# A fourth decay buffer for a state-space scan, placed in SBUF, and side work moved to later scans

## What is computed

```python
mod = silu(c) @ W_ada + b_ada;  shift, scale, gate = split(mod, 3)
h = layernorm(x, gamma, beta) * (1 + scale) + shift;  h = h[:, perm]
xm, z = split(h @ W_in, 2);  xm = silu(conv4(xm) + conv_b)          # 1024 channels
dtr, B, C = split(xm @ W_xp, [64, 80]);  dt = softplus(dtr @ W_dt + b_dt)
for t in rows:                                                       # state: 1024 channels x 16
    state = state * exp(dt_t * A) + (dt_t * x_t) * B_t;  y_t = sum_s state * C_t
out = x + gate * (((y + xm * D) * silu(z)) @ W_out)[inverse]
```

## Time and profile before

| | |
|---|---|
| median of 3 runs | 3013.91 us |
| the profiled execution | 3009.61 us, span 3007.8 us, mean granted TensorE clock 0.949 |
| DVE busy | 2466.3 us (82% of the span) |
| PE busy | 2648.0 us (88%) |
| POOL busy | 1883.4 us (63%) |
| ACT busy | 1621.8 us (54%) |
| stretch of the scans, 1030.7 to 2951 us | 1920.3 us, DVE busy in 1844.98, POOL 1676.82, PE 1633.54, ACT 1324.89 |

### The profile page before, as it was taken

One profiled execution on the slowest core, in us unless ns is written; L12 is line 12 of the kernel. 1 busy time (PEld: TensorE's weight loads), 2 busy tenths in 40 slices (PEclk: granted clock), 3 DMA queues, 4 the chain that ended last, 5 costly groups with the idle time before them and its releaser, 6 DMA issues. The chain is left out here.

```text
span 3007.8 us, 31819 instructions
## 1 busy us (share of the span) xinstructions
PE 2648.0 (88%) x10790; PEld 1499.2 (50%) x10790; DVE 2466.3 (82%) x3111; ACT 1621.8 (54%) x2444; POOL 1883.4 (63%) x822
## 2 busy tenths in 40 slices
PE   7999999999999877988988988988888897897974
PEld 3555555555555354554554554455455455454542
DVE  3566556666656599999999999999999998999993
ACT  1221322331332576776875875776676687586550
POOL 0131121222122396897998899799799799889991
PEclk9999999999999878999989999999999998998976
DMA  6102231231233444555664575665575566566653
GB/s 216 36 28 85 69 106 42 91 112 36 91 112 116 135 98 97 118 126 119 151 148 122 143 164 115 146 158 120 133 161 130 133 148 147 126 142 137 171 122 75
DMA packets 261604, 355.39 MB, mean 118 GB/s; under 512 B 21597, under 2 KB 115937, under 8 KB 261434
## 3 DMA queue, kind: packets, MB, share of 16 engines
q1 hardware_dynamic: 202024, 246.38, 26.8%
q0 software_dynamic: 55680, 105.93, 20.1%
q10 hardware_dynamic: 3730, 0.96, 0.2%
HBM read 215.56 MB, written 71.58 MB: 95 GB/s over the span
## 5 line engine op out<-in xcount | busy, mean ns | idle before, releaser
L2073 POOL TENSOR_TENSOR hs<-slots,b_wide 128x2048 f32<-128x2048 f32 x255 | 1270.5, 5011 | 142.8 <-PE bank L1589 142.6
L2267 DVE TENSOR_TENSOR_SCAN hs<-bank,hs 128x512 f32<-128x512 f32 x1024 | 1224.5, 1215 | 30.3 <-ACT bank L1846 25.3
L1846 ACT ACTIVATE bank<-dt,decay 128x512 f32<-128x512 f32 x1022 | 698.6, 691 | 540.7 <-DVE hs L2267 538.5
L1589 PE MATMUL bank<-ident,hs 128*128 128x128 f32 x4096 | 676.1, 295 | 240.1 <-DVE acc L2285 181.0
L1589 PEld LDWEIGHTS bank<-ident,hs 128*128 128x128 f32 x4096 | 515.1, 150 | 724.3 <-issue 264.0
L2285 DVE SCALAR_TENSOR_TENSOR acc<-bank,c_t,acc 128x512 f32<-128x512 f32 x772 | 566.4, 734 | 43.0 <-PE bank L1589 40.2
L1541 PE MATMUL bank<-h_t,w_in 128*128 128x512 f32 x1024 | 510.8, 608 | 1.4 <-ACT h_t L1764 1.2
L2121 POOL DMA_DIRECT2D acc<-scaled x252 | 291.2, 1155 | 49.2 <-DMA acc<-scaled 35.0
L982 POOL TENSOR_TENSOR y_rs<-y_var,mhalf 128x8 f32<-128x8 f32 x8 | 15.8, 1972 | 393.5 <-DVE y_var L355 393.5
L1641 PE MATMUL bank<-w_y,values 128*128 128x512 f32 x512 | 253.0, 600 | 1.3 <-DVE values L2389 1.3
L800 PE MATMUL bank<-z_t,w_k 128*128 128x512 f32 x512 | 223.0, 594 | 4.3 <-DVE k_t L1009 3.2
(11 more groups left out here) (180 smaller groups left out, 3344.3 us busy)
## 6 DMA issues: line engine op xcount, KB each, us to landing
b_wide<-b_rows SPq DMA_DIRECT2D x256, 256.0 KB, 3.6
acc<-scaled POOLq DMA_DIRECT2D x252, 256.0 KB, 5.3
w_in<-in_L_cond_W_in SPq DMA_DIRECT2D x128, 256.0 KB, 4.4
res<-in_x SPq DMA_DIRECT2D x8, 2048.0 KB, 10.0
h_tiles<-h_t SPq DMA_DIRECT2D x56, 256.0 KB, 2.8
h_in<-h_tiles SPq DMA_DIRECT2D x56, 256.0 KB, 4.1
x_rows<-w_part POOLq DMA_DIRECT2D x28, 512.0 KB, 6.8
x_rows<-res SPq DMA_DIRECT2D x6, 2048.0 KB, 7.3
```

The lines of the kernel that those rows point to most:

```text
L1589: last = nc.tensor.transpose(bank[:, j * P:(j + 1) * P], hs[:, slot, j, t * P:(t + 1) * P], ident[:, :])
L1846: nc.scalar.activation(decay_banks[N % 3][:, :], dt[:, H % 2, j, :], ACT.Exp, scale=g.decay[:, 4 * (H % 2) + j, s:s + 1]).then_inc(da_read ...
L2073: nc.gpsimd.tensor_tensor(hs[:, U % RING, :, :], slots[:, H % SLOTS, :, :], b_wide[:, U % B_RING, :].unsqueeze(1).to_broadcast([P, 4, CHUNK]),
L2267: nc.vector.tensor_tensor_scan(block, decay_banks[N % 3][:, :], block, 0.0, ALU.mult, ALU.add).then_inc(scanned, 1)
```

## The change

`decay_banks` gets a fourth entry, `decay_tile`, which lies in SBUF where the other three are PSUM banks. Since a unit has four scans, the fourth scan of every unit, 256 in all, reads its decay from SBUF, and the other three keep a bank of their own. ACT now issues the decay of scan n + 4 at step n; it still waits until scan n has ended. The addition to the second half's step sizes (`ADD_DT_AT`) moves on POOL from unit 7 to 9. ACT's `shift` moves from step 14 to 18, and the four normalisations, which stood together at 15, stand one each at 19, 20, 21 and 22, each behind its own column of `shift`. The transposes, the modulations and the first product by W_in follow by one or two steps, the second silu of z by one, and the first product waits for each modulated tile by itself instead of for the last three together. `raw`, the place of the moments, now lies in columns of `cols` that layer 0 has used up.

```diff
+DECAY_RING = 4
-H_AT = (21, 22, 22, 28)
+H_AT = (23, 24, 24, 28)
-XM_AT = (30, 33, 42, 51, 62, 63, 66, 69)
+XM_AT = (31, 33, 42, 51, 62, 63, 66, 69)
-SILU_Z_AT = (104, 2)
+SILU_Z_AT = (104, 3)
-NORM_AT = 15
-MOD_AT = (26, 27, 27, 33)
+NORM_AT = (19, 20, 21, 22)
+MOD_AT = (27, 28, 29, 33)
-ADD_DT_AT = (28, 7)
+ADD_DT_AT = (28, 9)
-SHIFT_AT = 14
+SHIFT_AT = 18
-        g.raw = sb("raw1", [P, CT, 6])
+        g.raw = g.cols[:, 0:6 * CT].rearrange("p (t s) -> p t s", t=CT)
-def rows_normed_by_act(nc, g, n, it):
-    need(nc.scalar, g.shift_ready, CT * n)
-    for t in range(CT):
-        nc.scalar.activation(g.rows[:, t, :], ...).then_inc(g.normed, 1)
+def rows_normed_by_act(nc, g, n, t):
+    need(nc.scalar, g.shift_ready, CT * (n - 1) + t + 1)
+    nc.scalar.activation(g.rows[:, t, :], ...).then_inc(g.normed, 1)
...
-        state_banks, decay_banks, work_banks = banks[0:2], banks[3:6], [banks[6], banks[7], banks[2]]
+        decay_tile = sb("decay_tile", [P, CHUNK])
+        state_banks, decay_banks, work_banks = banks[0:2], [*banks[3:6], decay_tile], [banks[6], banks[7], banks[2]]
...
-                    if stage == "xm" and m == 0:
-                        for i in range(KD)[-place.ring:]:
-                            need(pe, *read_by(place, "h", i))
                 for k in ks:
+                    if stage == "xm" and m == 0:
+                        need(pe, *read_by(place, "h", k))
...
-                need(act, scanned, N - 2)
-                nc.scalar.activation(decay_banks[N % 3][:, :], dt[:, H % 2, j, :], ACT.Exp,
+                need(act, scanned, N - (DECAY_RING - 1))
+                nc.scalar.activation(decay_banks[N % DECAY_RING][:, :], dt[:, H % 2, j, :], ACT.Exp,
...
-                    if N + 3 < BLOCKS * BATCH:
-                        decays(N + 3)
+                    if N + DECAY_RING < BLOCKS * BATCH:
+                        decays(N + DECAY_RING)
...
-                nc.vector.tensor_tensor_scan(block, decay_banks[N % 3][:, :], block, 0.0, ALU.mult, ALU.add).then_inc(scanned, 1)
+                nc.vector.tensor_tensor_scan(block, decay_banks[N % DECAY_RING][:, :], block, 0.0, ALU.mult, ALU.add).then_inc(scanned, 1)
```

More of the change, by code:

```diff
@@ L447, in rows_shift_by_act @@
         nc.scalar.activation(g.shift[:, t:t + 1], g.rs[:, t:t + 1], ACT.Copy, scale=g.mean_neg[:, t:t + 1]).then_inc(g.shift_ready, 1)
-def rows_normed_by_act(nc, g, n, it):
-    need(nc.scalar, g.shift_ready, CT * n)
-    for t in range(CT):
-        nc.scalar.activation(g.rows[:, t, :], g.rows[:, t, :], ACT.Identity, scale=g.rs[:, t:t + 1], bias=g.shift[:, t:t + 1]).then_inc(g.normed, 1)
+def rows_normed_by_act(nc, g, n, t):
+    need(nc.scalar, g.shift_ready, CT * (n - 1) + t + 1)
+    nc.scalar.activation(g.rows[:, t, :], g.rows[:, t, :], ACT.Identity, scale=g.rs[:, t:t + 1], bias=g.shift[:, t:t + 1]).then_inc(g.normed, 1)
 def rows_normed(nc, g, it):
@@ L1536, in project_in @@
                     need(pe, w_in_loaded[m % W_IN_RING], DMA * (loads + 1))
+                for k in ks:
                     if stage == "xm" and m == 0:
-                        for i in range(KD)[-place.ring:]:
-                            need(pe, *read_by(place, "h", i))
-                for k in ks:
+                        need(pe, *read_by(place, "h", k))
                     last = nc.tensor.matmul(work_bank(place, stage, m)[:, :], w_in[:, m % W_IN_RING, k, :], h_t[:, place.par, k, :],
@@ L1912, in turn @@
                             rows_shift_by_act(nc, g, b + 1, b + 1)
-                        if n == NORM_AT:
-                            rows_normed_by_act(nc, g, b + 1, b + 1)
+                        for t, at in enumerate(NORM_AT):
+                            if n == at:
+                                rows_normed_by_act(nc, g, b + 1, t)
                         for i, at in enumerate(MOD_AT):
@@ L1979, in first_chunk @@
                         diagonal(j + DIAG_RING)
+                decays(3)
                 for b in range(BATCH):
```

## The result

The changed kernel took 3452.88 us (median of four, 3447.14 to 3453.88) against 3013.41 us before in the same series: a ratio of 1.1454, 95% interval 1.1435 to 1.1472. The direction was right, the size was not: 440 us slower instead of 135.

What follows compares the result with a forecast made beforehand. DVE's queue was taken to bound layer 1's scans: 3009.6 us profiled, plus 167 of fourth-scan waits, less 25.3 and 7 of gains, gives 3144.3; with 4.3 for the median, 3148 us. Own range 3066 to 3204, with rivals to 3303.

Steps and rivals of the forecast that it cites:

- What bounds the kernel: Layer 1's scans: DVE's queue sets the pace, about 75 us idle in 1920.3; its waits count one for one.
- Two SBUF inputs: The 256 fourth scans keep 1.215 us bare, but contend with POOL's products, as two rows of plain DVE products and sums showed.
- The failed step: Fourth scans: one starting while a POOL product is under way is held until that product's end; 167 us after re-phasing.
- the walk's size: DVE's and POOL's queues walked through, each wait carried into later starts: 90 fourth scans wait, 167 us in all.
- How long a product holds POOL: A POOL row ends at its own end or the next start, whichever is first: 4.48 us for most products.
- POOL is held too: Fourth scans that start first hold POOL's products: 63 us in all, out of POOL's 240 us idle.
- DMA issues: On POOL beside DVE's two-SBUF-tile instructions: the issue is held, up to a scan's length, DVE is not; no cost.
- The gain of the buffer: ACT's decays one scan further ahead remove 25.3 us of scan waits; with 7 us at the additions, 32 us.
- The side work: Normalisations spread over steps 19 to 22 give 7 us at the additions; the sum at unit 9 and other moves cost nothing.
- the scan does not contend: Rival for the fourth scans: POOL reads between their reads, only the gain is left, 2982 us; 14 in 100.
- POOL becomes the bound: Rival: POOL's products, held by scans, come late and scans wait for inputs; 3250 us, 3 in 100.
- The waits don't re-phase: Rival: all 321 us of fourth scans' waits are paid, 3303 us; 8 in 100 between 3204 and this.

Runs made afterwards that it cites:

- e5_noread: The changed kernel with POOL's 255 large products of a unit replaced by POOL writing zeros to the same tiles: 3008.63 us (one run).
- e9_pad4: The changed kernel with four small POOL writes (128x24) before each product of a unit, each waiting for the one before: 3166.01 us (one run).
- e11_pad1: The changed kernel with one small POOL write (128x24) before each product of a unit, which the product waits for: 3197.07 us (one run).
- e7_issues: The changed kernel with POOL's DMA issue of a unit made as two issues of 64 partitions each: 3541.83 us (one run).
- e10_three7: The changed kernel with three PSUM decay banks and the second step sizes' sum back at unit 7: 3012.28 us, ratio 0.9997 to the kernel before.

## Why the prediction was right and wrong

**What bounds the kernel.** Right: the waits inside the scans came out nearly one for one in the span: 468 us of them, less 26 us of idle time gone, made 443 us.

**Two SBUF inputs.** Right in kind. Scans that meet no POOL product keep 1.2 us; held ones end 1.08 or 1.09 us behind a product; e5_noread shows that POOL's reading is the cause. The two rows of plain products were enough to forecast it for a scan.

**The failed step** is the sentence that a fourth scan "is held until that product's end". It is the first product's end only in 59 of 95 cases. Where POOL has its next product at hand, that goes first and the scan waits it out as well: 211 of the 468 us. The row that I took the rule from the earlier trace rows couldn't show it: behind POOL's product of 1026.53 stood a second that was not ready to go, since it waited for DVE itself. With the overtaking shut off, the walk's size appears: 161 us in 92 waits (e9_pad4) against the 167 us in 90 of the prediction. That it fits to 6 us is in part luck, since e11_pad1 has 192 us in 85. Of the 468 us the part up to the first product also grew, to 256. That each wait of 5 to 10 us puts DVE at another place against POOL would explain it, and so would the short reading of POOL's rows, below; neither was tried by itself.

**How long a product holds POOL.** Wrong in the reading: where two rows overlap, it is the start of the later one that isn't run yet, and not the end of the earlier. Taken to the rows' own ends, the fourth scans of the kernel before meet 145 products, with 366 us of rest, instead of the prediction's 125 and 321. If each of them also waits out every product dispatched within 0.11 us of the former's end, the same trace gives 643 us. Neither count carries the waits into the later starts, so they are no forecasts, but they show that the rows of before held the larger price.

**POOL is held too.** It is (a product of 5.27 us behind a scan, above), but as it waits 404 us for transposes in the changed kernel, nothing came of it.

**DMA issues.** From the earlier trace rows I took that DVE holds an issue while an issue doesn't hold DVE. The first half has more for it than two rows: of the 32 indirect issues of that line in the kernel before, the other 30 stood beside no DVE product of two SBUF tiles and took 0.95 to 1.09 us. The second half stands for the changed kernel: 47 fourth scans started while an issue and no product was there, and all took 1.20 to 1.22 us. This direction agrees with what the Trainium skill (SBUF — State Buffer, Who interferes with whom) infers, that a sum or product of DVE and descriptor generation need different interfaces of the shared pair; the rows of the first half differ from it. But e7_issues, with its 12 held scans, shows issues taking some part when a product follows them.

**The gain of the buffer.** 25.3 us of waits for decays are gone, as computed. The 7 us at the additions are not (39.1 to 40.5 us). e5_noread gives 34 us in all for what the prediction put at 32; it doesn't part the tile's share from that of POOL's shorter work.

**The side work.** That it costs nothing was right without the tile (0.3% faster) and wrong beside it (46 us, 33 of them from the sum that the prediction put at nothing). With three banks the additions' waits for transposes fall from 40.2 to 27.6 us, and to 26.5 with the sum at unit 7 (e10_three7). So the normalisations gave 13 us where the prediction said 7, but without the sum's move the scans' waits for POOL's products took it back (4.8 us before, 21.4 then).

**The rivals.** That the scan does not contend is refuted by the 95 held scans and e5_noread. *POOL becomes the bound* is out, since POOL waits 404 us for transposes. *The waits don't re-phase* had 3303 us for its end; the mechanism that the runs show, a waiter that loses its turn again, was not among them, and so the range ended 150 us too low.

**Left open.** Why a scan gets in at 33 of 38 ends where the next product is dispatched 0.2 to 0.62 us later behind one issue, but at only 4 of 26 behind two. What is shown is that in e9_pad4 and e11_pad1, where a product may only be dispatched after a completed wait on POOL, it got in at all 177 ends, 35 of them with the next product within 0.6 us. Whether the lower granted clock (0.891 against 0.949) cost anything was not tried; PE's busy time grew by 106 us, but DVE's waits for the transposes grew by 1.4 us only. A fourth bank in PSUM for the decays, with two work banks left, was not run.

## What to carry to other kernels

Before a tile moves from PSUM to SBUF, count the SBUF inputs of every DVE instruction that reads it: with two, each one is tied to POOL's reading instructions. Price such a wait not by one POOL instruction but by the run of them that POOL has ready; if it can't be avoided, try a small wait of POOL between two of them. And measure a buffer and the tables that were tuned with it apart: here one cost 13% and the other gained 0.3%.

## What was not expected of the hardware

In three kernels a DVE scan of two SBUF tiles that waits for POOL is overtaken by POOL's next reading instruction at 102 of 104 ends when this is dispatched within 0.11 us of the end, at 53 of them with a DMA issue between the two; waits of 10.6 us came of instructions of 4.5 us. A product shuts the scan out from its dispatch on, before it runs (13 scans of the changed kernel). With a single 128x24 write of POOL that the next product waits for, the scan was overtaken at 0 of 85 ends. When the scan gets in, it ends 1.09 us behind the product, 0.12 us less than its own 1.21 us.
